# Last attention: four maximum units of a group move to the score banks, copied by ScalarE and folded on GpSimd

## The chip, the cores and the metric

One Trainium2 core runs the whole program in one launch. The metric is the device time of that launch in microseconds. The kernel before was timed three times: 1482.65, 1487.79 and 1488.82 us, median 1487.79 us. Engines: TensorE (PE; PEld is its weight load), VectorE (DVE), ScalarE (ACT), GpSimd (POOL), SyncE (SP, which issues DMAs).

## The reference

The program is a two-layer decoder on x of 4 x 512 x 256, each sublayer followed by a layer norm: attention, cross attention and a mixture of experts, then causal attention with rotary embedding, cross attention over a context of 1601 keys, and a tree of leaves. Only the last cross attention ("xa" in the kernel) is touched:

```python
def _L1_xattn_ref(q, k, v, Wq, bq, Wk, bk, Wv, bv, Wo, bo):   # 16 heads of 16
    qh = (q @ Wq + bq).reshape(B, LQ, HEADS, D_K).transpose(0, 2, 1, 3)
    kh = (k @ Wk + bk).reshape(B, LKV, HEADS, D_K).transpose(0, 2, 1, 3)
    vh = (v @ Wv + bv).reshape(B, LKV, HEADS, D_K).transpose(0, 2, 1, 3)
    scores = jnp.einsum('bhqd,bhkd->bhqk', qh, kh) * scale
    attn = jax.nn.softmax(scores, axis=-1)
    out = jnp.einsum('bhqk,bhkd->bhqd', attn, vh)
    ...
```

Here q has 512 rows in each of 4 batches, k and v have 1601.

## The kernel before, in words

`heads_loop` runs the 64 heads (4 batches x 16) as 16 groups of four heads. Each group is worked on twice. The first pass finds an estimate of each query's largest score, which the softmax subtracts. The second pass computes scores again, transposed (keys on partitions, all 512 queries along the row), takes the exponential, and multiplies by the values.

**First pass, the maximum units.** The 1601 keys are cut at 0, 512, 1024, 1473 and 1601 (`cut`). A unit is (head, block of 128 queries, cut): one bf16 matmul of 512 or 449 columns (`unit` of the tensor block, L2045) into one of three PSUM banks (banks 4 to 6), and one VectorE reduction from that bank to one column (L2194). For the last 128 keys one unit takes all four query blocks (L2039, L2187). That makes 52 units for a group: 32 of 512 columns, 16 of 449, 4 of the rest. A unit may start when the unit three places before it has been reduced. When a group's units are done, VectorE reduces the 64 partial results of each partition to 16 negated maxima (`of_cuts`, L2200), GpSimd splits them into two bf16 parts (`parts`, L1994 and L1996), PE transposes them (`shift`, L2054), ScalarE copies them out (`row`, L2154), and a DMA writes them as two extra rows under the queries, so that the second pass subtracts them in its matmul.

**Second pass.** For each of 13 blocks of 128 keys ("kt"), `scores` (L2069) computes two pairs of heads, four matmuls a pair, into one of two score banks, each two PSUM banks wide (`S_PS(p)`, p even or odd: banks 0 and 1, or 2 and 3). ScalarE takes the exponential of a pair at once, 128x1024 (L2145). A pair p may start when exponential p-2 is done. `values` (L2085) multiplies the block before by its values, four heads side by side in bank 7, with float32 operands. After a group's last values ScalarE copies the output to OT (`output`, L2135).

**Row halves.** Heads 0 and 2 of a group lie on partitions from 0, heads 1 and 3 on partitions from 64 (`base(h)`). Matmuls of 48 or 50 rows on different halves can run side by side; matmuls on the same half follow each other. The values use all 128 rows.

**Order.** PE's order is written by `group(g, ...)` of the tensor block: in every kt two scores, one values, and between them, by `due(point, count)`, maximum units of the groups ahead. Group g carries units 18 to 51 of group g+1 and then units 0 to 17 of group g+2, 52 in 39 points, four in a kt. The shift of group g+1 stands after unit 4 of group g+2 (`BEHIND`). Group 0 carries 65 units, group 14 has no group g+2 and carries 34, group 15 none. VectorE runs the units in the same order, with `of_cuts(g-1)` after unit 0 of group g. GpSimd's queue holds for each group the reload of values (`reload_v`, L1968) and then `parts`. SP reloads queries and keys when a group's scores are done. The order of units is that of `units_of_cuts`.

Of the kernel before, what the change touches and what calls it, by code (L numbers as in the profile page):

```python
# [34 lines left out]
P = 128  # L35
# [1735 lines left out]


LEFT = 128


def units_of_cuts(cuts):
# [51 lines left out]
def heads_loop(nc, env, name, hb, OT, keys=None, queries=None):  # L1828
# [13 lines left out]
    CUTS = len(cut) - 1  # L1842
    if causal:
        units = [(h, qt, 0) for h, qt in CAUSAL_UNITS]
    else:
        units = units_of_cuts(CUTS)
    U = len(units)
    R1 = UNIT_BANKS
    EARLY = U if causal else 18
    LEAD = U if causal else 5  # L1850
# [13 lines left out]

    def at(g, n):

        return g * U + n + (max(g - 1, 0) + (n > BEHIND and g > 0))

    def shift_at(g):

# [12 lines left out]
    with ExitStack() as c:  # L1883
# [17 lines left out]
        if not causal:  # L1901
            s_cuts = sem(name + "_cuts")
            s_mrow = sem(name + "_mrow")
            s_xb = sem(name + "_xb")
        s_step = sem(name + "_step")
        s_mh = sem(name + "_mh")
        s_2 = sem(name + "_2")
# [9 lines left out]
        with nc.Block() as block:  # L1917
# [44 lines left out]
            @block.gpsimd  # L1962
            def _(pool):
                def load_v(g, u):
                    full = NK // P
                    if causal and g % G == 0:
                        keys.landed(pool, g // G)
                    pool.dma_start(Vg[:, u, 0:full, :],  # L1968
                                   hb.vp[g][0:full * P, :].rearrange("(k p) n -> p k n", p=P)).then_inc(s_v[u], 16)
                    if full < KT:  # L1970
                        pool.dma_start(Vg[0:rows(full), u, full, :], hb.vp[g][full * P:NK, :]).then_inc(s_v[u], 16)

                def reload_v(g, u):
# [24 lines left out]
                if not causal:
                    parts(0)
                    for t in range(T):  # L2000
                        last = pool.tensor_tensor(env.x[:, t, :], env.x[:, t, :], env.w["x_bo"], ALU.add)
                    last.then_inc(s_xb, 1)
                    pool.wait_ge(s_xb, 1)
                    for g in range(1, GROUPS):
                        if 2 <= g <= GROUPS - R + 1:
                            reload_v(g - 2, (g - 2) % R)
                        parts(g)
                    return
                for n in keys.rest:
                    keys.split.pool_lo(pool, n)  # L2010
                pool.wait_ge(keys.split.s_lo, keys.rest[-1] + 1)
                for u in range(hb.RING, R):
                    hb.ones(pool, u).then_inc(s_ones, 1)
                pool.wait_ge(s_ones, R - hb.RING)
                for g in range(GROUPS):
                    for kt in range(KT):
                        triangle(g, kt)
                        if kt == 1 and 1 <= g <= GROUPS - R:
                            reload_v(g - 1, (g - 1) % R)

            @block.tensor
            def _(pe):
# [7 lines left out]
                def unit(g, u, n, first):  # L2030

                    if n == 0:
                        pe.wait_ge(hb.s_kq[u], 16 * hb.LOADS * (first + 1))
                    bank_free(at(g, n))
                    h, qt, e = units[n]
                    tile, to, out = base(h), place(h, 0), bank(at(g, n))
                    if qt is None:
                        for t in range(TB):
                            last = pe.matmul(out[:, t * LEFT:(t + 1) * LEFT],  # L2039
                                             hb.q(u)[tile:tile + HALF, to, t * P:(t + 1) * P],  # L2040
                                             hb.k(u)[tile:tile + HALF, to, cut[e]:NK], start=True, stop=True,
                                             tile_position=(tile, 0))
                    else:
                        width = (qt + 1) * P if causal else cut[e + 1] - cut[e]
                        last = pe.matmul(out[:, 0:width], hb.q(u)[tile:tile + HALF, to, qt * P:(qt + 1) * P],  # L2045
                                         hb.k(u)[tile:tile + HALF, to, cut[e]:cut[e] + width], start=True, stop=True,
                                         tile_position=(tile, 0))
                    last.then_inc(s_1, 1)
# [6 lines left out]
                              start=True, stop=True).then_inc(s_1, 1)  # L2055

                def scores(g, u, kt, h, first):
                    p = (kt * G + h) // 2
                    if p == 0:
                        pe.wait_ge(s_mq[u], 32 * (first + 1))  # L2060
                    if g or p >= 2:
                        pe.wait_ge(s_exp, g * PAIRS + (p - 1))
                    r = rows(kt)
                    w_ = L - q0(kt)
                    out = lambda j: S_PS(p)[0:r, j, 0:w_]
                    for half in range(2):
                        for j in range(2):
                            tile, to, depth = base(j), place(h, half), HALF + 2 * (half == 0)
                            last = pe.matmul(out(j), hb.k(u)[tile:tile + depth, to, kt * P:kt * P + r],  # L2069
                                             hb.q(u)[tile:tile + depth, to, q0(kt):L], start=(half == 0),  # L2070
                                             stop=(half == 1), tile_position=(tile, 0))
                    last.then_inc(s_2, 1)

                def values(g, u, kt, first):

                    r = rows(kt)
                    if kt == 0:
                        pe.wait_ge(s_v[u], 16 * VLOADS * (first + 1))
                        pe.wait_ge(s_ot, g + 1)
                    if causal:  # L2080
                        pe.wait_ge(s_tri, g * KT + (kt + 1))
                    else:
                        pe.wait_ge(s_exp, g * PAIRS + (kt + 1) * (G // 2))
                    for h in range(G):
                        last = pe.matmul(O_PS[h * VW:(h + 1) * VW, q0(kt):L], Vg[0:r, u, kt, h * VW:(h + 1) * VW],  # L2085
                                         Pr[0:r, (u * KT + kt) % PR, h, 0:L - q0(kt)], start=(kt == 0), stop=(kt == KT - 1),
                                         tile_position=(0, h * VW))
                    last.then_inc(s_pv, 1)

                def group(g, u, first, before, ahead):  # L2090
# [5 lines left out]
                    for kt in range(KT):  # L2096
                        for turn in range(TURNS):
# [14 lines left out]
                                    shift(g + 1)  # L2112
                            if ahead == 1 and point == LAST_POINT:
                                shift(g + 1)

                for n in range(U):
                    if not causal and n in project_at:
                        block_, k = project_at[n]
                        queries.project(pe, block_, queries.ps(block_), (k,))
# [12 lines left out]
            def _(act):  # L2132
# [4 lines left out]
                def group(g, u, before):  # L2137
                    for kt in range(KT):
# [1 line left out]
                        r = rows(kt)  # L2140
                        w_ = L - q0(kt)
                        for h in range(0, G, 2):
                            p = (kt * G + h) // 2
                            act.wait_ge(s_2, g * PAIRS + (p + 1))
                            act.activation(Pr[0:r, (u * KT + kt) % PR, h:h + 2, 0:w_], S_PS(p)[0:r, :, 0:w_], ACT.Exp,  # L2145
                                           scale=SCALE).then_inc(s_exp, 1)
                        if kt == 0 and before:
                            output(g - 1)
                        if not causal and kt == ROW_AT and g + 1 < GROUPS:
                            row(g + 1)  # L2150

# [27 lines left out]
            def _(dve):  # L2179
                def unit(g, n):  # L2180

                    h, qt, e = units[n]
                    dve.wait_ge(s_1, at(g, n) + 1)
                    src = bank(at(g, n))
                    col = h % 2 * COLS // 2 + h // 2 * TB
# [8 lines left out]
                        dve.tensor_reduce(part[:, g % 2, col + qt, e:e + 1], src[:, 0:cut[e + 1] - cut[e]], AX, ALU.max).then_inc(s_1free, 1)  # L2194

                def of_cuts(g):
                    dve.wait_ge(s_1free, reduced(at(g, U - 1)))
                    if g >= 2:
                        dve.wait_ge(s_mh, g - 1)
                    dve.tensor_reduce(mx[:, g % 2, :], part[:, g % 2, :, :], AX, ALU.max, negate=True).then_inc(s_cuts, 1)  # L2200
# [11 lines left out]
                    dve.tensor_copy(mrow[:, :], M_PS(g)).then_inc(s_1free, 1)  # L2212

                for g in range(GROUPS):
                    for n in range(U):
                        if g or not causal:
                            unit(g, n)
                        if causal and (g, n) in rest_after:
# [592 lines left out]
```

## Time and profile before

| | |
|---|---|
| median of three runs | 1487.79 us |
| the profiled execution's own time | 1489.09 us |
| its span (first to last instruction) | 1487.1 us |
| PE, DVE, ACT, POOL busy, share of the span | 92%, 71%, 52%, 22% |
| xa units' reductions (L2194), 768 | 462.7 us busy, 662 ns each |
| xa exponentials (L2145), 416 | 403.4 us busy, 1021 ns each |

The xa loop runs from about 861 to 1400 us. Read its rows by group: from one `of_cuts` to the next is one period of the loop. Busy shares of PE are upper bounds, since the ends of matmuls are modelled and matmuls overlap; where PE stands at nearly 100% it must be read instruction by instruction.

### The profile page before, as it was taken

The numbers are of one execution on the slowest core, as the hardware profiler recorded it, in microseconds if no ns is written. First come the engines' busy times: TensorE is split into PE (matmuls) and PEld (weight loads), VectorE is DVE, ScalarE is ACT, GpSimd is POOL, SyncE is SP. The second block draws the span as 40 slices with busy tenths as digits, with TensorE's granted clock in tenths as the row PEclk, the third lists the DMA queues.
The fourth block names the chain that finished last, engine by engine and source line by source line (L and its number), as shares of the span: only waits on it lengthen the run. The fifth ranks groups of instructions, "written<-read, shape, count | busy, mean of one in ns | idle before, by whom it ended". The sixth has DMA issues, their size and how long they took to land. (4 is left out here: it accounts for less than half of the span.)

```text
span 1487.1 us, 24888 instructions
## 1 busy us (share of the span) xinstructions
PE 1369.3 (92%) x9358; PEld 762.8 (51%) x9358; DVE 1059.4 (71%) x2351; ACT 774.8 (52%) x1067; POOL 321.7 (22%) x407
## 2 busy tenths in 40 slices
PE   6898899989999989869998889999999999999996
PEld 3565578756899886423335422333333333333285
DVE  4887466662122128968994799999999999997077
ACT  2344266631111112336763316888888888888754
POOL 3110322243000017743335440000000000000011
PEclk9999799999999999969999869999999999999999
DMA  9548533346889842674422650343222343220001
GB/s 341 194 134 246 171 122 128 122 165 226 299 279 302 272 152 79 215 222 143 131 66 60 177 164 2 85 102 80 67 67 68 86 101 80 68 67 2 1 1 57
DMA packets 152841, 198.68 MB, mean 134 GB/s; under 512 B 15723, under 2 KB 124799, under 8 KB 152594
## 3 DMA queue, kind: packets, MB, share of 16 engines
q1 hardware_dynamic: 141004, 165.34, 36.7%
q0 software_dynamic: 9200, 29.64, 6.4%
q10 hardware_dynamic: 2518, 2.13, 0.4%
q8 instruction: 74, 1.21, 0.4%
q14 instruction: 45, 0.37, 0.1%
HBM read 136.08 MB, written 60.70 MB: 132 GB/s over the span
## 5 line engine op out<-in xcount | busy, mean ns | idle before, releaser
L2194 DVE TENSOR_REDUCE xa_part<-psum 128x1 f32<-128x512 f32 (+1 forms) x768 | 462.7, 662 | 20.4 <-PE psum L2045 18.6
L2145 ACT ACTIVATE xa_P<-psum 128x1024 f32<-128x1024 f32 (+1 forms) x416 | 403.4, 1021 | 103.3 <-PE psum L2069 102.6
L2069 PE MATMUL psum<-sa_Q,xa_K 48*128 48x512 bf16 (+3 forms) x1664 | 267.0, 381 | 3.9 <-DMA sa_Q<-xa_mrow 2.9
L2045 PE MATMUL psum<-xa_K,sa_Q 48*128 48x512 bf16 (+1 forms) x768 | 239.3, 388 | 4.4 <-DVE xa_part L2194 1.5
L2085 PE MATMUL psum<-xa_P,xa_V 128*32 128x512 f32 (+1 forms) x1664 | 222.6, 607 | 0.4 <-ACT xa_P L2145 0.4
L2045 PEld LDWEIGHTS psum<-xa_K,sa_Q 48*128 48x128 bf16 x768 | 59.2, 94 | 232.5 <-DVE xa_part L2194 160.8
L2069 PEld LDWEIGHTS psum<-sa_Q,xa_K 48*128 48x128 bf16 (+3 forms) x1664 | 105.6, 97 | 68.7 <-ACT xa_P L2145 20.7
L2191 DVE CUSTOM_DVE_ANT_0 psum<-psum,cf_sb 128x512 f32<-128x512 f32 (+1 forms) x240 | 111.5, 520 | 18.3 <-PE psum L2045 17.5
L1334 PEld LDWEIGHTS psum<-xtT,wgu 128*128 128x128 f32 x992 | 115.5, 192 | 5.8 <-issue 4.6
L1334 PE MATMUL psum<-xtT,wgu 128*128 128x128 f32 x992 | 115.9, 275 | 1.4 <-issue 0.8
L2145 ACT ACTIVATE sa_P<-psum 128x1024 f32<-128x1024 f32 (+3 forms) x128 | 83.4, 702 | 49.1 <-PE psum L2069 49.1
L1483 DVE TENSOR_TENSOR ht<-sgt,psum 128x512 f32<-128x512 f32 x31 | 21.3, 688 | 114.1 <-ACT sgt L1386 114.1
L1386 ACT ACTIVATE sgt<-psum 128x512 f32<-128x512 f32 x31 | 18.5, 597 | 132.6 <-PE psum L1334 132.6
L212 POOL TENSOR_TENSOR t_rstd<-t_ve,mhalf 128x2 f32<-128x2 f32 (+1 forms) x36 | 27.6, 768 | 229.3 <-DVE t_ve L207 229.1
L2045 PE MATMUL psum<-sa_K,sa_Q 48*128 48x512 bf16 (+1 forms) x240 | 64.7, 321 | 12.1 <-PEq L1556 5.5
L2069 PE MATMUL psum<-sa_Q,sa_K 50*128 50x256 bf16 (+7 forms) x512 | 63.9, 308 | 4.0 <-DMA sa_Q<-sa_mrow 2.6
L1994 POOL CAST xa_mh<-xa_mx 128x16 bf16<-128x16 f32 x16 | 3.1, 197 | 293.0 <-DVE xa_mx L2200 266.8
L2085 PEld LDWEIGHTS psum<-xa_P,xa_V 128*32 128x32 f32 (+1 forms) x1664 | 32.9, 108 | 53.5 <-issue 50.6
L634 PE MATMUL psum<-a_in_sb,xT_sb 128*128 128x384 f32 x128 | 48.5, 526 | 12.9 <-DMA xT_sb<-in_xT 10.1
L1215 PE MATMUL psum<-xT_sb,big_weights 128*128 128x512 f32 x128 | 58.8, 614 | 0.7 <-PEq L937 0.7
L1981 POOL TENSOR_SCALAR_AFFINE_SELECT sa_P<-sa_P 128x512 f32<-128x512 f32 x64 | 40.6, 634 | 86.6 <-ACT sa_P L2145 86.6
L1344 PE MATMUL psum<-wdn,ht 128*128 128x256 f32 x248 | 58.7, 380 | 0.6 <-DVE yt L1490 0.6
(250 smaller groups left out, 2140.7 us busy)
## 6 DMA issues: line engine op xcount, KB each, us to landing
wgu<-in_f_gu SPq DMA_DIRECT2D x31, 1024.0 KB, 6.3
xa_K<-kx SPq DMA_DIRECT2D x192, 100.1 KB, 4.9
wdn<-in_f_dn SPq DMA_DIRECT2D x31, 512.0 KB, 6.5
vx<-xv_v SPq DMA_DIRECT2D x48, 256.0 KB, 3.3
xa_V<-vx POOLq DMA_DIRECT2D x16, 768.0 KB, 6.5
sa_Q<-qs SPq DMA_DIRECT2D x64, 96.0 KB, 2.3
sa_K<-ks SPq DMA_DIRECT2D x64, 96.0 KB, 2.3
sa_Q<-qx SPq DMA_DIRECT2D x64, 96.0 KB, 2.3
```

Source lines behind the costliest of these rows:

```text
L212: pool.tensor_tensor(self.rstd[:, u, :], self.ve[:, u, :], self.env.mhalf[:, 0:self.tc], ALU.pow).then_inc(self.s_rstd, 1)
L634: pe.matmul(o, env.xT[:, k, t * P:(t + 1) * P], w["a0_in"][:, k, cols], start=(k == 0), stop=False)
L1215: last = pe.matmul(o, w[name][:, k, f * P:(f + 1) * P], env.xT[:, k, c * L:(c + 1) * L], start=(k == 0), stop=(k == KD - 1))
L1334: last = pe.matmul(GU(j)[:, f * P:(f + 1) * P], wgu[:, u, k, f * P:(f + 1) * P], xtT[:, u, k, :], start=(k == 0), stop=(k == KD - 1))
L1344: last = pe.matmul(Y_PS[:, 0:D], ht[:, u, f, :], wdn[:, u, f, :], start=(f == 0), stop=(f == FC - 1))
L1981: pool.affine_select(square, square, [[0, G], [1, P]], ALU.is_ge, 0.0, base=0, channel_multiplier=-1).then_inc(s_tri, 1)
L2045: last = pe.matmul(out[:, 0:width], hb.q(u)[tile:tile + HALF, to, qt * P:(qt + 1) * P], hb.k(u)[tile:tile + HALF, to, cut[e]:cut[e] + widt ...
L2069: last = pe.matmul(out(j), hb.k(u)[tile:tile + depth, to, kt * P:kt * P + r], hb.q(u)[tile:tile + depth, to, q0(kt):L], start=(half == 0), ...
L2085: last = pe.matmul(O_PS[h * VW:(h + 1) * VW, q0(kt):L], Vg[0:r, u, kt, h * VW:(h + 1) * VW], Pr[0:r, (u * KT + kt) % PR, h, 0:L - q0(kt)], ...
L2145: act.activation(Pr[0:r, (u * KT + kt) % PR, h:h + 2, 0:w_], S_PS(p)[0:r, :, 0:w_], ACT.Exp, scale=SCALE).then_inc(s_exp, 1)
L2191: dve.tensor_tensor_reduce(src[:, 0:k1], src[:, 0:k1], env.later[:, L - k1:L], 1.0, -3e38, ALU.add, ALU.max, mx[:, g % 2, col + qt:col + q ...
L2194: dve.tensor_reduce(part[:, g % 2, col + qt, e:e + 1], src[:, 0:cut[e + 1] - cut[e]], AX, ALU.max).then_inc(s_1free, 1)
```

## The change

In the xa loop, the units (head 0 or 1, query block 0, cut 0 or 1), four of the 52, are taken out of the list for all groups but group 0, which keeps its 52. Their matmuls are computed as two pairs in the score banks, a pair after kt 0 and a pair after kt 1 of the group before (`fold_units`). Each pair takes a place in the order of pairs, so that the group has 28 instead of 26. ScalarE copies each pair, 128x1024, to SBUF, over constants that are no longer used (`fold`). GpSimd folds: the second copy b against the first copy a as a + max(b - a, 0), in three instructions; then the upper half of each head's 512 against the lower half, and once more, which leaves 128 per head. One VectorE reduction takes these to the four partial results, before `of_cuts`. The list of units is 48 long, so `due` spreads 48 over 39 points.

```diff
+        first_units = units_of_cuts(CUTS)
+        units = [(h, qt, e) for h, qt, e in first_units if not (h < 2 and qt == FOLD_QT and e < 2)]
...
+    FOLDS = () if causal else FOLD_AFTER
+    PAIRS += len(FOLDS)
+    pair_of = lambda g, kt, h: (kt * G + h) // 2 + sum(after < kt for after in FOLDS) * (g + 1 < GROUPS)
...
+                def folds(g):
+                    for e in range(2):
+                        pool.wait_ge(s_exp, (g - 1) * PAIRS + pair_of(g - 1, FOLD_AFTER[e], 2) + 2)
+                    a, steps, wide = fold[:, 0], 3 * FOLDINGS * (g - 1), BANK
+                    b = fold[:, 1]
+                    for n in range(FOLDINGS):
+                        pool.tensor_tensor(b, b, a, ALU.subtract).then_inc(s_fold, 1)
+                        pool.wait_ge(s_fold, steps + 3 * n + 1)
+                        pool.tensor_scalar(b, b, 3e38, 0.0, ALU.min, ALU.max).then_inc(s_fold, 1)
+                        pool.wait_ge(s_fold, steps + 3 * n + 2)
+                        pool.tensor_tensor(a, a, b, ALU.add).then_inc(s_fold, 1)
+                        if n < FOLDINGS - 1:
+                            pool.wait_ge(s_fold, steps + 3 * n + 3)
+                            wide //= 2
+                            a, b = fold[:, 0, :, 0:wide], fold[:, 0, :, wide:2 * wide]
...
+                        folds(g)
                         parts(g)
...
+                def fold_units(g, u, e, first):
+
+                    p = pair_of(g, FOLD_AFTER[e], 2) + 1
+                    if e == 0:
+                        pe.wait_ge(hb.s_kq[(u + 1) % R], 16 * hb.LOADS * (first + (u + 1) // R + 1))
+                    pe.wait_ge(s_exp, g * PAIRS + (p - 1))
+                    v = (u + 1) % R
+                    for h in range(2):
+                        tile, to = base(h), place(h, 0)
+                        last = pe.matmul(S_PS(p)[:, h, 0:BANK], hb.q(v)[tile:tile + HALF, to, FOLD_QT * P:(FOLD_QT + 1) * P],
+                                         hb.k(v)[tile:tile + HALF, to, cut[e]:cut[e + 1]], start=True, stop=True,
+                                         tile_position=(tile, 0))
+                    last.then_inc(s_2, 1)
...
+                        if kt in FOLDS and ahead >= 1:
+                            fold_units(g, u, FOLDS.index(kt), first)
...
                         if kt == 0 and before:
                             output(g - 1)
+                        if kt in FOLDS and g + 1 < GROUPS:
+                            p = pair_of(g, kt, 2) + 1
+                            if g:
+                                act.wait_ge(s_cuts, g + 1)
+                            act.wait_ge(s_2, g * PAIRS + (p + 1))
+                            act.activation(fold[:, FOLDS.index(kt)], S_PS(p), ACT.Copy).then_inc(s_exp, 1)
...
                 def of_cuts(g):
-                    dve.wait_ge(s_1free, reduced(at(g, U - 1)))
+                    dve.wait_ge(s_1free, reduced(at(g, count(g) - 1)))
+                    if g:
+                        dve.wait_ge(s_fold, 3 * FOLDINGS * g)
+                        dve.tensor_reduce(part[:, g % 2, FOLD_QT:FOLD_QT + COLS // 2 + 1:COLS // 2, 0:2],
+                                          fold[:, 0, :, 0:BANK >> (FOLDINGS - 1)].rearrange("p h (e k) -> p h e k", e=2),
+                                          AX, ALU.max).then_inc(s_folded, 1)
+                        dve.wait_ge(s_folded, g)
```

PE in a middle group before, from the last values of the group before (the row of 32x512 x4, sa_Q holds the queries, L2069 the scores, L2045 and L2039 the units):

```order
L2085 MATMUL psum<-xa_P,xa_V 32x512 x4
L2045 MATMUL psum<-xa_K,sa_Q 128x449
L2039 MATMUL psum<-xa_K,sa_Q 128x128 x4
L2069 MATMUL psum<-sa_Q,xa_K 128x512 x4
L2039 MATMUL psum<-xa_K,sa_Q 128x128 x4
L2069 MATMUL psum<-sa_Q,xa_K 128x512 x4
L2045 MATMUL psum<-xa_K,sa_Q 128x512
L2085 MATMUL psum<-xa_P,xa_V 32x512 x4
L2045 MATMUL psum<-xa_K,sa_Q 128x449
L2045 MATMUL psum<-xa_K,sa_Q 128x512
L2069 MATMUL psum<-sa_Q,xa_K 128x512 x4
```

The same place now (L2128 values, L2098 scores, L2074 units, L2112 the new pairs):

```order
L2128 MATMUL psum<-xa_P,xa_V 32x512 x4
L2074 MATMUL psum<-xa_K,sa_Q 128x449
L2112 MATMUL psum<-xa_K,sa_Q 128x512 x2
L2098 MATMUL psum<-sa_Q,xa_K 128x512 x4
L2074 MATMUL psum<-xa_K,sa_Q 128x512
L2098 MATMUL psum<-sa_Q,xa_K 128x512 x4
L2074 MATMUL psum<-xa_K,sa_Q 128x512 x2
L2128 MATMUL psum<-xa_P,xa_V 32x512 x4
L2074 MATMUL psum<-xa_K,sa_Q 128x449
L2112 MATMUL psum<-xa_K,sa_Q 128x512 x2
L2098 MATMUL psum<-sa_Q,xa_K 128x512 x4
```

A new pair stands in front of the scores of kt 1 and another in front of those of kt 2. The second scores of kt 1 and of kt 2 are now the pairs that have to wait for the new copies.

ScalarE around the end of a group before (L2145 exponentials, 65x1024 is the last kt, then kt 0 of the next group, its output copy L2135, and L2154 the row of maxima):

```order
L2145 ACTIVATE xa_P<-psum 128x1024 x4
L2145 ACTIVATE xa_P<-psum 65x1024 x2
L2145 ACTIVATE xa_P<-psum 128x1024 x2
L2135 ACTIVATE OT<-psum 128x512
L2145 ACTIVATE xa_P<-psum 128x1024 x18
L2154 ACTIVATE xa_mrow<-psum 32x128
```

And now (L2190 exponentials, L2180 output, L2199 the new copies into the region of cf_sb, L2205 the row):

```order
L2190 ACTIVATE xa_P<-psum 65x1024 x2
L2190 ACTIVATE xa_P<-psum 128x1024 x2
L2180 ACTIVATE OT<-psum 128x512
L2199 ACTIVATE cf_sb<-psum 128x1024
L2190 ACTIVATE xa_P<-psum 128x1024 x2
L2199 ACTIVATE cf_sb<-psum 128x1024
L2190 ACTIVATE xa_P<-psum 128x1024 x16
L2205 ACTIVATE xa_mrow<-psum 32x128
```

The first copy stands between the output copy and the exponentials of kt 1, the second between those of kt 1 and those of kt 2.

## Rows read from the trace of the kernel before

**Rows 1.** Windows: a middle group, most of group 15, group 0.
```profile
core 0: us, PE busy (x) PEld busy (x) DVE busy (x) ACT busy (x) POOL busy (x), PEclk, DMA share, GB/s
934.60:966.40 31.80, 31.60 (x275) 11.37 (x273) 31.27 (x54) 25.81 (x29) 2.02 (x5) 1.00 0.32 75
1377.90:1400.00 22.10, 21.43 (x170) 4.07 (x168) 0.00 (x0) 20.27 (x22) 0.00 (x0) 1.00 0.00 1
894.00:935.00 41.00, 39.21 (x295) 12.50 (x298) 38.12 (x65) 25.95 (x28) 2.61 (x6) 0.94 0.07 21
```
**Rows 2.** Timeline, POOL: the parts of maxima of two groups.
```profile
start us, us, engine line op out<-in xcount [idle before <-releaser]
1080.23 0.20 POOL L1994 CAST xa_mh<-xa_mx 128x16 bf16<-128x16 f32 x1 [17.70 <-DVE xa_mx L2200]
...
1112.04 0.20 POOL L1994 CAST xa_mh<-xa_mx 128x16 bf16<-128x16 f32 x1 [17.71 <-DVE xa_mx L2200]
1112.33 0.21 POOL L1996 TENSOR_TENSOR xa_mh<-xa_mx,xa_mh 128x16 bf16<-128x16 f32 x1
```
**Rows 3.** Lines by form, 934 to 1348 us (13 groups): VectorE and ScalarE.
```profile
line engine op names shapes xcount | busy us, mean ns | idle before us <-releasers
L2194 DVE TENSOR_REDUCE xa_part<-psum 128x1 f32<-128x512 f32 x416 | 261.6, 681 | 0.0
L2194 DVE TENSOR_REDUCE xa_part<-psum 128x1 f32<-128x449 f32 x209 | 128.2, 624 | 7.0 <-PE psum L2045 5.7
...
L2145 ACT ACTIVATE xa_P<-psum 128x1024 f32<-128x1024 f32 x313 | 303.4, 1021 | 71.8 <-PE psum L2069 71.5
```
**Rows 4.** Timeline, PE, one kt of a middle group.
```profile
1098.56 1.06 PE L2085 MATMUL psum<-xa_P,xa_V 128*32 128x512 f32 x8
1099.55 0.39 PE L2045 MATMUL psum<-xa_K,sa_Q 48*128 48x449 bf16 x2
1099.76 0.81 PE L2069 MATMUL psum<-sa_Q,xa_K 50*128 50x512 bf16 x5
...
1100.96 0.64 PE L2085 MATMUL psum<-xa_P,xa_V 128*32 128x512 f32 x4
```
**Rows 5.** Timeline, PE, at a group's end: last values, kt 1, first values.
```profile
1091.32 1.06 PE L2085 MATMUL psum<-xa_P,xa_V 65*32 65x512 f32 x8
...
1093.18 0.60 PE L2069 MATMUL psum<-sa_Q,xa_K 50*128 50x512 bf16 x3
...
1093.74 0.64 PE L2085 MATMUL psum<-xa_P,xa_V 128*32 128x512 f32 x4
```
**Rows 6.** Timeline, ACT, the same stretch (kt 0, output, kt 1).
```profile
1090.81 1.94 ACT L2145 ACTIVATE xa_P<-psum 128x1024 f32<-128x1024 f32 x2 [0.45 <-PE psum L2069]
1092.64 0.60 ACT L2135 ACTIVATE OT<-psum 128x512 f32<-128x512 f32 x1
1093.26 1.94 ACT L2145 ACTIVATE xa_P<-psum 128x1024 f32<-128x1024 f32 x2
```
**Rows 7.** Timeline, group 15, without units: ACT and the PE loads behind it.
```profile
1377.66 3.88 ACT L2145 ACTIVATE xa_P<-psum 128x1024 f32<-128x1024 f32 x4
1379.67 0.12 PEld L2069 LDWEIGHTS psum<-sa_Q,xa_K 50*128 50x128 bf16 x4 [0.67 <-ACT xa_P L2145]
```
**Rows 8.** Timeline around the shift of a middle group.
```profile
1111.77 0.21 DVE L2200 TENSOR_REDUCE xa_mx<-xa_part 128x16 f32<-128x64 f32 x1
...
1113.32 0.23 PE L2054 MATMUL psum<-cb_sb,xa_mh 128*32 128x128 bf16 x1 [0.20 <-DVE xa_part L2194]
```
**Rows 9.** Lines by form, POOL, whole program.
```profile
L1981 POOL TENSOR_SCALAR_AFFINE_SELECT sa_P<-sa_P 128x512 f32<-128x512 f32 x64 | 40.6, 634 | 86.6 <-ACT sa_P L2145 86.6
L353 POOL TENSOR_TENSOR sqk_whole<-sqk_ta,sqk_tb 128x512 f32<-128x512 f32 x16 | 22.2, 1392 | 9.8 <-DVE sqk_tb L334 9.5
L2001 POOL TENSOR_TENSOR x_sb<-x_sb,x_bo_sb 128x256 f32<-128x256 f32 x16 | 10.9, 715 | 0.0
```
**Rows 10.** Waits, 900 to 1390 us: PE's loads of units behind VectorE.
```profile
PEld psum L2045 <- DVE xa_part L2194: 136.2, 171, 0.8
```

More of the change, by code:

```diff
@@ L1773 @@
 LEFT = 128
+FOLD_QT = 0
+FOLD_AFTER = (0, 1)
+FOLDINGS = 3
 def units_of_cuts(cuts):
@@ L1844, in heads_loop @@
         units = [(h, qt, 0) for h, qt in CAUSAL_UNITS]
+        first_units = units
     else:
-        units = units_of_cuts(CUTS)
-    U = len(units)
+        first_units = units_of_cuts(CUTS)
+        units = [(h, qt, e) for h, qt, e in first_units if not (h < 2 and qt == FOLD_QT and e < 2)]
+    U0, U = len(first_units), len(units)
+    count = lambda g: U if g else U0
+    FOLDS = () if causal else FOLD_AFTER
+    PAIRS += len(FOLDS)
+    pair_of = lambda g, kt, h: (kt * G + h) // 2 + sum(after < kt for after in FOLDS) * (g + 1 < GROUPS)
     R1 = UNIT_BANKS
@@ L1865, in at @@
     def at(g, n):
-        return g * U + n + (max(g - 1, 0) + (n > BEHIND and g > 0))
+        return n if g == 0 else U0 + (g - 1) * U + n + (g - 1) + (n > BEHIND)
     def shift_at(g):
@@ L1904, in heads_loop @@
             s_xb = sem(name + "_xb")
+            s_fold = sem(name + "_fold")
+            s_folded = sem(name + "_folded")
+            fold = env.cf[:, CF_FIRST:CF_FIRST + 4 * BANK].rearrange("p (e h k) -> p e h k", e=2, h=2)
         s_step = sem(name + "_step")
@@ L2034, in unit @@
                     bank_free(at(g, n))
-                    h, qt, e = units[n]
+                    h, qt, e = units[n] if g else first_units[n]
                     tile, to, out = base(h), place(h, 0), bank(at(g, n))
@@ L2057, in scores @@
                 def scores(g, u, kt, h, first):
-                    p = (kt * G + h) // 2
+                    p = pair_of(g, kt, h)
                     if p == 0:
@@ L2082, in values @@
                     else:
-                        pe.wait_ge(s_exp, g * PAIRS + (kt + 1) * (G // 2))
+                        pe.wait_ge(s_exp, g * PAIRS + pair_of(g, kt, 2) + 1)
                     for h in range(G):
@@ L2114, in group @@
                                 shift(g + 1)
-                for n in range(U):
+                        if kt in FOLDS and ahead >= 1:
+                            fold_units(g, u, FOLDS.index(kt), first)
+                for n in range(U0):
                     if not causal and n in project_at:
@@ L2142, in group @@
                         for h in range(0, G, 2):
-                            p = (kt * G + h) // 2
+                            p = pair_of(g, kt, h)
                             act.wait_ge(s_2, g * PAIRS + (p + 1))
@@ L2180, in unit @@
                 def unit(g, n):
-                    h, qt, e = units[n]
+                    h, qt, e = units[n] if g else first_units[n]
                     dve.wait_ge(s_1, at(g, n) + 1)
@@ L2214, in _ @@
                 for g in range(GROUPS):
-                    for n in range(U):
+                    for n in range(count(g)):
                         if g or not causal:
```

## The prediction

> **What bounds the kernel now.** I read the windows by stage first, then the lines by form of the xa loop, then single rows of the timeline, because here the shares don't decide. In a middle group VectorE is busy 31.27 of 31.80 us and PE 31.60, both full; ScalarE 25.81, GpSimd 2.02 [rows 1]. The period is 1112.04 - 1080.23 = 31.81 us [rows 2]. The waits list PE's loads behind the units' reductions with 136.2 us [rows 10]; taken alone it says that VectorE is the bound and that every unit taken from it pays. Three things speak against that. First, VectorE's own idle time in 13 groups is 7.0 us, and it ends on PE [rows 3]: it is VectorE that waits in the end. Second, PE has no hole in a kt. It is: values at 1098.56, next matmul at 1099.55, scores from 1099.76, next values at 1100.96 [rows 4]. That is 2.40 us: 1.0 us of values, the rest for 8 score matmuls and 4 units, 12 matmuls on two row halves, so 6 slots one behind the other. 1100.96 - 1099.55 = 1.41; a matmul of 512 columns takes its half 0.22 us (four of scores on two halves take 0.44, as 1099.76 less 1099.55 is one slot of 0.21), so 6 slots are 1.32 and 0.09 is left for the change to values. Third, the loads wait for the values in front of them anyway: group 15 has no units at all, and its loads wait 0.67 us "for ScalarE" in the same place [rows 7]. So PE paces, at 13 x 2.41 = 31.3 us, and 0.5 us comes on top around the shift, where PE does wait for a bank of VectorE's (0.20 us idle at 1113.32) [rows 8].
>
> ScalarE is the other half of PE's loop. There are two score banks, and a pair may start only when the exponential two pairs back is done. Four exponentials in a row take 3.88 us, 0.97 each; the first after a gap counts 1.02 [rows 3, 7]. At kt 0 the output copy already fills ScalarE's gap: kt 0's two from 1090.81, output 1092.64 to 1093.24, kt 1's two from 1093.26, without idle time [rows 6].
>
> **The change part by part.**
>
> Four units less on VectorE, 14 groups. A reduction of 512 columns costs one step of (261.6 / 416 =) 0.63 us, so 2.5 us a group leave, and one reduction of 256 elements comes. Its price lies between 0.21 us (64 elements, [rows 8]) and 0.63; I take 0.4 and 0.15 for its two handshakes. VectorE is relieved by about 2 us a group, which off the path is worth nothing by itself.
>
> PE's work: nothing is taken away. The same four matmuls run, two side by side: 2 slots of 0.22 in kt 0 and 1. The units that remain are 48 in 13 kt, three or four in each. Three units still take 6 slots (4 + 2 on one half, 4 + 1 on the other), so a kt with three is not shorter. Where three fall on one half it takes 7, 0.22 us more. Taking units 0, 2, 3 and 4 out of the list breaks the alternation of halves: by the heads in the list I count this in kt 9 and kt 10, and once after kt 1, where two units of one half stand in a row behind the values. That makes +0.6 us a group. Around the shift the 0.5 us may go (VectorE has slack) or double (the fold's reduction stands in front of `of_cuts`): -0.5 to +0.5, I take -0.1. Remainder: +0.5 a group, from -0.5 to +1.2.
>
> The two copies: this is the main term. A copy of 128x1024 from PSUM is the shape of the exponential, so 1.02 us [rows 3]. No row shows this copy to SBUF; the output copy, half its size, takes 0.60 [rows 6], which bounds it by 1.2 above and by 0.97 below. I follow the group that ends at 1091.32 [rows 5, 6]:
> - Copy 1 waits in ScalarE's queue behind the output copy: 1093.28 to 1094.30. Its matmuls were ready at about 1092.9.
> - The exponentials of kt 1 wait behind it: from 1094.33 instead of 1093.26, the second ends at 1096.27.
> - The second scores of kt 1 need copy 1's bank. They start at 1094.30 + 0.07 = 1094.37 (the 0.07: exponential ends 1377.66 + 1.94 = 1379.60, PE's load at 1379.67 [rows 7]) instead of 1093.18 [rows 5]. PE issues in order, so units and values behind them wait too. Then 0.44 of scores, one slot of units, 0.09: values at 1095.12 instead of 1093.74. Late by 1.38.
> - Values to 1096.12, a short unit and the second pair on the same half 0.41, 0.16 to its end: 1096.69. ScalarE has been idle since 1096.27 and starts copy 2 at 1096.80, until 1097.82.
> - The first scores of kt 2 run meanwhile; the second need copy 2's bank: 1097.89, plus 0.44, 0.22 and 0.09: values at 1098.64. Before, they stood one kt after 1093.74: 1096.15. Late by 2.49.
> - Kt 2's exponentials end at 1099.80, before the second scores of kt 3 ask for the bank (about 1100.3). From here on PE paces again, and ScalarE has 0.4 us a kt, so nothing is won back, for PE has no slack.
>
> So 2.45 us a group (2.2 to 2.9 with the bounds of the copy). With the remainder: 2.95 x 14 groups (1 to 14) = 41.3 us.
>
> Group 0 is another case: 65 units in 41 us, VectorE busy 38.12 [rows 1], so VectorE paces at 5 units a kt, 3 us, and two exponentials and a copy fit into 3 us. Four units less are 2.5 us, the fold's reduction costs some of it: -1.5 us (-2.5 to +2.5). Group 15 has no copies. The first 52 units stay.
>
> GpSimd: nine instructions a group on 1024, 512 and 256 elements. Two inputs: 512 take 1.39, 256 take 0.72 [rows 9], so 1024 take 2.8: 4.9 us a series, 9.8 for the two series. The third kind has one input; no row shows it. One-input affine selects take 0.63 for 512 [rows 9], so 2.2 a series; as dear as two inputs it would be 4.9. Handshakes 9 x 0.09 [rows 2]. Together 12.8 to 15.5 us from the end of copy 2 at 1097.8. `of_cuts` ran at 1111.77 [rows 8] and comes about 2.5 us later and one turn (a third of a kt) earlier: 1113.9. There are 16.1 us, so it is hidden, at worst with 0.6 us left. The Trainium skill (GPSIMD Engine Reference, section 3.1, "Elementwise — side-by-side cycle accounting") has about 2.6 cycles an element for two inputs and 1.03 for one; by its figures the nine would take an estimated 9.3 us and a start each, shorter than by the rows, and still hidden. The values' reload stands in GpSimd's queue before the folds and isn't delayed; `parts` stands behind them and needs `of_cuts` anyway.
>
> The other waits: ScalarE's wait for `of_cuts` of the group is met a group earlier; the wait for the next group's keys was met when its units began.
>
> **Sum.** +41.3 - 1.5 = +39.8. Against the profiled execution: 1489.1 + 39.8 = 1528.9; it lies 1.3 us over the median of the three runs, so 1527.6 for a median, 1528. Its own range: 14 x (2.2 - 0.5) - 2.5 = +21 to 14 x (2.9 + 1.2) = +57, which I narrow to 1513 to 1542 since not all ends meet.
>
> **Rivals.**
> - VectorE paces after all. Then units taken from it pay and the waits of PE are slack. For it: 31.27 of 31.80 us busy, 136.2 us of waits. Against it: its idle time ends on PE. It would save 2.0 us of reductions less 0.15, down to ScalarE's floor: 28 x 1.0 + 0.6 + 0.25 and the gaps, about 30.0. So -1.8 x 15 = -27 us: 1461. This is the faster side; it decides as soon as PE's matmuls can go on under the copies. Chance 0.08.
> - The copies' waits are half taken up (the units standing in front of the scores run during them, the shift's 0.5 us goes and the halves cost nothing): the two cancel nearly. 14 x (1.0 - 0.5) = +7 and less: 1485 to 1495. It needs a second score bank free when copy 1 runs, and there is none. Chance 0.05.
> - GpSimd is late. If the nine take 18.5 us (inputs slowed by VectorE's traffic, which no row shows), `of_cuts` waits 2.4 us, three banks fill, PE stops: 14 x 2.4 = 34 more: 1562. Chance 0.10.
> - PE's clock falls in the new holes. Group 15 has ScalarE's holes in every kt and the granted clock is 1.00; at the low clock of group 0's beginning it is below, 0.94 over the group [rows 1]. If two kt a group ran at 1.2 instead of 2.4 GHz, each would cost up to its own 2.4 us again; by half of that, 14 x 2.4 = 34 more: 1562. Chance 0.04. The Trainium skill (TensorE: Matmul & The Clock Gate, "A second HAM failure mode: psum-queue depth-cycling") tells of a clock that swings where PE idles shortly between groups of matmuls while it cycles through PSUM; the row of group 15 doesn't bear it out.
>
> **Chances and range.** Forecast 0.73, the rivals 0.08, 0.05, 0.10, 0.04. A change under 0.5%, 7.4 us, can't be told from none. Faster 0.09, same 0.05, slower 0.86. The range must leave out no more than 0.2: 1509 to 1547 leaves out the first two rivals and most of the last two, which hold 0.25 with the nearer ends inside.
>
> **What would show it.** Right: the exponentials' count per group unchanged, two copies of about 1.02 us behind output and behind kt 1; PE idle about 1 us before the second scores of kt 1 and kt 2, ended by ScalarE's copy; values 3.8, 3.5 us apart at the group's start and 2.4 after; VectorE busy about 29 of 35 us a group; period 34.5 to 35.2. GpSimd's last fold ends before VectorE's reduction of it asks. Wrong: a period under 31.8 with VectorE still above 97% (first rival); VectorE's idle time ended by GpSimd (third); PEclk under 1.00 in the loop (fourth). If the values stand 2.4 us apart at kt 1 and 2, the main term is wrong.

## The result, and the profile after

Slower: median 1521.79 us against 1486.68 us, ratio 1.0241, 95% interval 1.0222 to 1.0260, +35.1 us. The forecast was 1528, +39.8. The profiled execution took 1521.9 us, its span 1520.1 us against 1487.1.

The windows of a whole middle group, of group 14 and of group 0, after (columns as in [rows 1]):

```profile
894.00:935.00 41.00, 38.61 (x310) 12.10 (x308) 37.26 (x64) 29.42 (x32) 15.07 (x14) 1.00 0.22 54
964.50:999.20 34.70, 33.30 (x275) 10.59 (x273) 29.81 (x50) 27.57 (x32) 12.87 (x13) 1.00 0.30 72
1380.70:1411.90 31.20, 29.93 (x244) 8.13 (x242) 15.96 (x27) 25.88 (x30) 11.23 (x11) 1.00 0.01 2
```

A middle group takes 34.68 us instead of 31.82. No engine is full any more: PE has 1.4 us without work, VectorE 4.9. PEclk is 1.00, so the holes did not cost clock. VectorE's lines by form over groups 1 to 13, to set beside [rows 3]:

```profile
L2245 DVE TENSOR_REDUCE xa_part<-psum 128x1 f32<-128x512 f32 x364 | 237.7, 686 | 54.0 <-PE psum L2074 49.9
L2245 DVE TENSOR_REDUCE xa_part<-psum 128x1 f32<-128x449 f32 x208 | 125.4, 618 | 7.6 <-PE psum L2074 7.5
L2251 DVE TENSOR_REDUCE xa_part<-cf_sb 128x4 f32<-128x256 f32 x13 | 5.3, 411 | 0.0
```

Its idle time rose from 7 us to over 60, and ends on PE. VectorE was relieved, and the relief turned into waiting. Where the time went stands in the timeline of PE at a group's end, the place of [rows 5]. A stretch is the time from the start of one kt's values (L2128) to that of the next:

```profile
1099.61 1.06 PE L2128 MATMUL psum<-xa_P,xa_V 65*32 65x512 f32 x8
1100.61 0.36 PE L2074 MATMUL psum<-xa_K,sa_Q 48*128 48x449 bf16 x1
1100.61 0.57 PE L2112 MATMUL psum<-xa_K,sa_Q 48*128 48x512 bf16 x2
1101.08 0.61 PE L2098 MATMUL psum<-sa_Q,xa_K 50*128 50x512 bf16 x4
...
1102.48 0.61 PE L2098 MATMUL psum<-sa_Q,xa_K 50*128 50x512 bf16 x4 [0.58 <-ACT cf_sb L2199]
...
1103.24 1.06 PE L2128 MATMUL psum<-xa_P,xa_V 128*32 128x512 f32 x8
...
1104.24 0.57 PE L2112 MATMUL psum<-xa_K,sa_Q 48*128 48x512 bf16 x2
...
1105.99 0.61 PE L2098 MATMUL psum<-sa_Q,xa_K 50*128 50x512 bf16 x4 [0.71 <-ACT cf_sb L2199]
...
1106.75 1.06 PE L2128 MATMUL psum<-xa_P,xa_V 128*32 128x512 f32 x8
```

and of ScalarE (to [rows 6]):

```profile
1100.91 0.60 ACT L2180 ACTIVATE OT<-psum 128x512 f32<-128x512 f32 x1
1101.38 1.05 ACT L2199 ACTIVATE cf_sb<-psum 128x1024 f32<-128x1024 f32 x1
1102.29 1.98 ACT L2190 ACTIVATE xa_P<-psum 128x1024 f32<-128x1024 f32 x2
1104.91 1.02 ACT L2199 ACTIVATE cf_sb<-psum 128x1024 f32<-128x1024 f32 x1 [0.65 <-PE psum L2112]
1105.83 1.94 ACT L2190 ACTIVATE xa_P<-psum 128x1024 f32<-128x1024 f32 x2
```

Copy 1 ends at 1102.43, and the second scores of kt 1 start at 1102.48; copy 2 ends at 1105.93, and those of kt 2 start at 1105.99. Values stand 3.63 and 3.51 us apart there (forecast 3.80 and 3.52), 2.41 before. The shorter first one is ScalarE's overlap: the start after an instruction comes 0.1 us before its end (1100.91 to 1101.38, 1101.38 to 1102.29), which I had counted only between the two exponentials of a kt. PE itself stands idle for 0.58 and 0.71 us, not for the 1 us that the prediction gave as a sign; beside the hole stand the new pair's own matmuls, 0.47 us with a unit (1100.61 to 1101.08).

GpSimd's folds, after:

```profile
1106.08 2.36 POOL L2016 TENSOR_TENSOR cf_sb<-cf_sb 128x1024 f32<-128x1024 f32 x1 [3.42 <-ACT cf_sb L2199]
1108.54 1.03 POOL L2018 TENSOR_SCALAR cf_sb<-cf_sb 128x1024 f32<-128x1024 f32 x1
1109.66 2.36 POOL L2020 TENSOR_TENSOR cf_sb<-cf_sb 128x1024 f32<-128x1024 f32 x1
...
1116.83 0.74 POOL L2020 TENSOR_TENSOR cf_sb<-cf_sb 128x256 f32<-128x256 f32 x1
```

and VectorE's reduction of them:

```profile
1121.63 0.41 DVE L2251 TENSOR_REDUCE xa_part<-cf_sb 128x4 f32<-128x256 f32 x1
```

The nine take 11.5 us, from 1106.08 to 1117.57, and end 4.1 us before VectorE's reduction of them starts, without idle time in front of it. They are hidden.

### The profile page after: what moved, and what is told of

Read it like the earlier page. It is cut to its first block and busy times, and to the rows that moved or that the text cites. A ratio compares the mean times of both kernels' runs of the same rounds, so it can differ in the third digit from the quotient of the medians.

```text
span 1520.1 us, 25081 instructions
## 1 busy us (share of the span) xinstructions
PE 1384.3 (91%) x9358; PEld 748.6 (49%) x9358; DVE 1036.3 (68%) x2306; ACT 800.5 (53%) x1097; POOL 484.1 (32%) x542
## 5 line engine op out<-in xcount | busy, mean ns | idle before, releaser
L2245 DVE TENSOR_REDUCE xa_part<-psum 128x1 f32<-128x512 f32 (+1 forms) x708 | 433.4, 661 | 76.5 <-PE psum L2074 71.2
L2190 ACT ACTIVATE xa_P<-psum 128x1024 f32<-128x1024 f32 (+1 forms) x416 | 403.9, 1024 | 104.3 <-PE psum L2098 104.0
L2098 PE MATMUL psum<-sa_Q,xa_K 50*128 50x512 bf16 (+3 forms) x1664 | 284.5, 381 | 22.6 <-ACT cf_sb L2199 18.6
L2074 PE MATMUL psum<-xa_K,sa_Q 48*128 48x512 bf16 (+1 forms) x708 | 232.4, 384 | 4.0 <-PEq L2327 1.0
L2128 PE MATMUL psum<-xa_P,xa_V 128*32 128x512 f32 (+1 forms) x1664 | 222.5, 607 | 0.4 <-ACT xa_P L2190 0.4
L2074 PEld LDWEIGHTS psum<-xa_K,sa_Q 48*128 48x128 bf16 x708 | 61.9, 95 | 214.7 <-DVE xa_part L2245 171.8
L2098 PEld LDWEIGHTS psum<-sa_Q,xa_K 50*128 50x128 bf16 (+3 forms) x1664 | 93.4, 96 | 113.1 <-ACT cf_sb L2199 33.4
L2190 ACT ACTIVATE sa_P<-psum 128x1024 f32<-128x1024 f32 (+3 forms) x128 | 83.4, 702 | 48.0 <-PE psum L2098 48.0
L2016 POOL TENSOR_TENSOR cf_sb<-cf_sb 128x1024 f32<-128x1024 f32 (+2 forms) x45 | 65.5, 1456 | 67.5 <-ACT cf_sb L2199 65.2
L2074 PE MATMUL psum<-sa_K,sa_Q 48*128 48x512 bf16 (+1 forms) x240 | 64.3, 319 | 12.1 <-PEq L1556 5.5
L1406 POOL DMA_DIRECT2D yg<-yt x31 | 16.8, 543 | 182.7 <-DVE yt L1490 182.7
L1980 POOL DMA_DIRECT2D xa_V<-vx x16 | 17.3, 1083 | 171.6 <-PE psum L2128 167.1
L2098 PE MATMUL psum<-sa_Q,sa_K 50*128 50x256 bf16 (+7 forms) x512 | 63.6, 307 | 4.2 <-DMA sa_Q<-sa_mrow 2.9
L2020 POOL TENSOR_TENSOR cf_sb<-cf_sb 128x1024 f32<-128x1024 f32 (+2 forms) x45 | 65.7, 1459 | 3.7
L2128 PEld LDWEIGHTS psum<-xa_P,xa_V 128*32 128x32 f32 (+1 forms) x1664 | 32.8, 108 | 64.1 <-issue 60.0
```

The lines of the kernel that those rows point to most:

```text
L2016: pool.tensor_tensor(b, b, a, ALU.subtract).then_inc(s_fold, 1)
L2020: pool.tensor_tensor(a, a, b, ALU.add).then_inc(s_fold, 1)
```

## The experiments

The starts of the values, read instruction by instruction from each trace, give the length of each stretch. In us, for a middle group, counted from its first values to those of the next group ("last" is the stretch in which the next group's copy 1 lies, 0-1 the one with copy 2; the shift lies in 7-8):

| kernel | 0-1 | 1-2 | 2-7 (sum) | 7-8 | 8-9 | 9-10 | 10-12 (sum) | last | group | median us | ratio to before (95%) |
|---|---|---|---|---|---|---|---|---|---|---|---|
| before | 2.41 | 2.41 | 12.09 | 2.69 | 2.59 | 2.41 | 4.82 | 2.42 | 31.82 | | |
| after | 3.51 | 2.49 | 12.24 | 2.82 | 2.59 | 2.59 | 4.82 | 3.63 | 34.68 | 1521.8 | 1.0241 (1.0222 to 1.0260) |
| e1 | 2.41 | 2.41 | 12.09 | 2.42 | 2.42 | 2.41 | 4.82 | 2.42 | 31.37 | 1478.8 | 0.9948 (0.9934 to 0.9963) |
| e2 | 2.38 | 2.49 | 12.24 | 2.64 | 2.59 | 2.59 | 4.81 | 2.41 | 32.15 | 1487.2 | 1.0003 (0.9993 to 1.0012) |
| e3 | 2.40 | 2.37 | 12.38 | 2.64 | 2.40 | 2.46 | 4.84 | 2.40 | 31.88 | 1483.8 | 0.9970 (0.9960 to 0.9980) |
| e4 | 3.53 | 2.41 | 12.09 | 2.69 | 2.59 | 2.41 | 4.82 | 3.64 | 34.16 | 1517.8 | 1.0205 (1.0190 to 1.0220) |

The rows' sums differ from the group by rounding. Each ratio compares with the kernel before, run beside that experiment. e1, e2, e3 and e5 leave part of the maxima out of the computation; of these only the times are used.

**e1_light_reduce: VectorE alone lighter.**

```diff
-src[:, 0:cut[e + 1] - cut[e]]
+src[:, 0:64 if g and h < 2 and qt == 0 and e < 2 else cut[e + 1] - cut[e]]
```

> The kernel before; only VectorE's reductions of the four units (head 0 or 1, query block 0, cut 0 or 1) of groups 1 to 15 read 64 of their 512 columns (those maxima are then over fewer keys). PE, ScalarE and the order are the same. Theory (PE paces, VectorE only around the shift): between no change and the 0.5 us a group of the shift, 0 to -7 us. Rival (VectorE paces): a reduction of 64 columns takes about 0.2 us instead of 0.63, so -1.7 us a group, -24 to -26 us.

Measured -0.5%, some 9 us (1478.8 against 1487.5). The four reductions fell to 0.22 us each, 1.8 us a group less for VectorE. VectorE's lines by form over groups 1 to 13:

```profile
L2194 DVE TENSOR_REDUCE xa_part<-psum 128x1 f32<-128x512 f32 x364 | 228.3, 681 | 0.0
L2194 DVE TENSOR_REDUCE xa_part<-psum 128x1 f32<-128x449 f32 x208 | 127.5, 623 | 21.0 <-PE psum L2045 20.5
...
L2194 DVE TENSOR_REDUCE xa_part<-psum 128x1 f32<-128x64 f32 x52 | 10.4, 220 | 3.2 <-PE psum L2045 3.2
```

Its idle time is 24.2 us instead of 7.0. Of each group only the two stretches around the shift moved, 5.28 to 4.84 us; all others kept their length to the hundredth. So VectorE holds PE back around the shift, by 0.44 us, and nowhere else. In 13 groups that is 5.7 us; the rest of the 9 lies outside them and is not explained here. The rival "VectorE paces" would have had -24 us.

**e2_drop4: the four units gone, nothing in their place.** (`FOLDS = ()`, no `folds(g)`.)

> The four units are left out of groups 1 to 15 altogether: no matmuls, no copies, no fold, 48 units in the changed kernel's order (their maxima are stale). Theory: a kt with three units takes the same six slots as one with four, and the disturbed order of row halves costs up to 0.6 us a group, the shift gives back up to 0.5: a middle group 31.6 to 32.1 us, the whole -5 to +3 us, though a thirteenth of the units is gone. Rival (VectorE paces): -2.5 us a group, -37 us. A count of PE's matmuls alone: two slots of 0.22 us a group, -6 us.

Measured 1.0003, with four matmuls and four reductions fewer in each group. The middle group even grew by 0.33 us. Group 0 shortened by 2.3 us (40.39 to 38.09): 1.7 us from its second stretch on, where VectorE paces, and 0.6 us in its first, which differs between traces with the same units too (4.62 us before, 4.35 in e4). A kt with three units takes 2.38 to 2.50 us, one with four 2.41: it is not shorter by a slot of 0.22.

**e3_drop4_turns: as e2, row halves in strict turn.** (The 48 units are listed even head, odd head, even head, ...)

> As e2_drop4, but the 48 units are listed with the row halves in strict turn (head even, head odd, ...). Theory of the halves: against e2_drop4 0.3 to 0.6 us a group less, -4 to -8 us, so -4 to -12 us against before; kt 9 and kt 10 fall from 2.6 to 2.4 us. Rival (halves cost nothing): the same as e2_drop4.

Measured 1483.8, against 1487.2 of e2. Stretch 8-9 fell from 2.59 to 2.40 us, 9-10 from 2.59 to 2.46 and 1-2 from 2.49 to 2.37; 2-7 rose by 0.14. On balance the order of the halves costs 0.27 us a group, half of what I had put for it.

**e4_copies_only: all 52 units on VectorE, pairs and copies added, nothing folded.** (`units = first_units`; no `folds(g)`; no reduction of the fold.)

> All 52 units stay on VectorE, and the two new pairs with their copies are added; nothing is folded and nothing reads the copies. Theory (copies and two score banks stall PE): 2.45 us a group at the first two kt, perhaps a bit more around the shift, +34 to +42 us against before, most of the changed kernel's loss; values 3.6 and 3.5 us apart at kt 0 and 1. Rival (the loss is of GpSimd, the fold's reduction and the order of units): +0 to +10 us.

Measured +2.05%, 30 us at the medians, a little under what I expected. The group is before's, hundredth by hundredth, except for the two stretches with copies: +1.22 and +1.12, together 2.35 us (31.82 to 34.16). This is 82% of the changed kernel's 2.86 us a group, with GpSimd, fold and order of units taken out. PE waits in the same place for the same reason:

```profile
969.51 0.41 PE L2111 MATMUL psum<-xa_K,sa_Q 48*128 48x512 bf16 x2
...
971.09 0.61 PE L2097 MATMUL psum<-sa_Q,xa_K 50*128 50x512 bf16 x4 [0.52 <-ACT cf_sb L2198]
```

**e5_short_copies: the copies take 64 columns of each half.**

```diff
-act.activation(fold[:, FOLDS.index(kt)], S_PS(p), ACT.Copy)
+act.activation(fold[:, FOLDS.index(kt), :, 0:64], S_PS(p)[:, :, 0:64], ACT.Copy)
```

> The changed kernel, but each copy takes 64 of the 512 columns of both halves (the fold then works on old data). Nothing else moves. Theory (it is the length of the copy between a pair and the scores two places on): a copy of 128 elements takes about 0.3 us instead of 1.02; the wait before the second scores of kt 1 falls from 0.6 us to nothing, that of kt 2 to about 0.1; of 2.35 us a group about 1.3 go, the two slots of the pairs and a rest stay: -18 us against the changed kernel, about 1504. Rival (the place in PE's order costs, not the copy): the same as the changed kernel, 1522.

Measured 1501.8 us (ratio to before 1.0105, 1.0079 to 1.0131), group 33.19 us, so 20 us of 35 gone. ScalarE and PE at copy 2:

```profile
995.78 0.28 ACT L2199 ACTIVATE cf_sb<-psum 128x128 f32<-128x128 f32 x1 [0.44 <-PE psum L2112]
996.21 1.94 ACT L2190 ACTIVATE xa_P<-psum 128x1024 f32<-128x1024 f32 x2 [0.16 <-PE psum L2098]
```
```profile
995.11 0.57 PE L2112 MATMUL psum<-xa_K,sa_Q 48*128 48x512 bf16 x2
995.39 0.72 PE L2098 MATMUL psum<-sa_Q,xa_K 50*128 50x512 bf16 x4
...
996.11 0.61 PE L2098 MATMUL psum<-sa_Q,xa_K 50*128 50x512 bf16 x4
```

The copy is 0.28 us and PE's second scores start 0.05 us behind its end, 996.06. They still wait, but less, which the waits of PE's loads for the copies show (us in all, times, longest), first in the changed kernel, then in e5:

```profile
PEld psum L2098 <- ACT cf_sb L2199: 31.9, 28, 1.2
```
```profile
PEld psum L2098 <- ACT cf_sb L2199: 9.7, 27, 0.4
```

The two stretches are 2.76 and 2.89 us. So the stretch follows the copy's length: 0.74 us less of copy gives 0.75 and 0.74 us less of stretch. Against e2, where nothing is copied (2.38 and 2.41), 0.86 us a group are left. The prediction put 0.44 of that down to the pairs' own matmuls; no run here separates them from the rest of the wait.

**e6_after_1_2: pairs behind kt 1 and 2** (`FOLD_AFTER = (1, 2)`).

> The changed kernel with the pairs behind kt 1 and 2 instead of 0 and 1, away from the output copy. In the copies' run kt 0 cost 1.23 us and kt 1 1.12 us. Theory: the output copy adds only the difference, so 2 x 1.12: -0.1 to -0.3 us a group, -1 to -5 us against the changed kernel. Rival (the output copy in front is what makes copy 1 dear): -0.5 us a group or more, -8 to -15 us.

A miss. 1523.9 us (1.0251, 1.0227 to 1.0274), the group 34.69 us as before the move. The two stretches are 3.51 and 3.73, where e2 without copies has 2.38 and 2.49, so 1.13 and 1.24 us. Taken with the changed kernel (1.22 behind kt 0, 1.13 behind kt 1) and with e7 below (1.24 behind kt 2, 1.16 behind kt 4), the price goes with the place. Copy 1 did get 0.09 us cheaper away from the output copy, as the theory had it, and copy 2 got 0.11 dearer behind kt 2. So the output copy is at most 0.1 us of the price; why kt 2 is the dearer place I did not isolate.

**e7_after_2_4: pairs behind kt 2 and 4.**

> The changed kernel with the pairs behind kt 2 and 4. The nine folds take 11.5 us there and end 4.1 us before VectorE asks. Copy 2 now ends about 7.1 us later. Theory (the rival of the late GpSimd, made true): VectorE waits about 3 us for GpSimd in each group, the three unit banks fill, PE loses 2 to 3 us of it: +28 to +42 us against the changed kernel, 1550 to 1564. Other theory (VectorE's slack takes the wait up): 1518 to 1526.

The direction was right, the size was not, twice the 42 us that the theory had as its most: 1610.2 us, ratio 1.0838 (1.0810 to 1.0866), +88 us against the changed kernel. VectorE waits for GpSimd as foreseen:

```profile
1116.48 0.42 DVE L2251 TENSOR_REDUCE xa_part<-cf_sb 128x4 f32<-128x256 f32 x1 [3.38 <-POOL cf_sb L2020]
```

and PE, out of unit banks, stands still 2.99 us. Then something comes on top, in the timeline of PE and the windows (columns as in [rows 1]):

```profile
1117.75 0.60 PE L2074 MATMUL psum<-xa_K,sa_Q 48*128 48x512 bf16 x1 [2.99 <-DVE xa_part L2245]
...
1119.91 1.94 PE L2128 MATMUL psum<-xa_P,xa_V 128*32 128x512 f32 x8
```
```profile
1112.00:1116.00 4.00, 2.76 (x23) 0.74 (x19) 1.10 (x2) 2.96 (x3) 3.58 (x6) 1.00 0.00 0
1116.00:1119.00 3.00, 1.25 (x6) 0.36 (x7) 2.48 (x6) 0.00 (x0) 0.80 (x3) 0.71 0.01 3
1119.00:1122.00 3.00, 3.00 (x15) 0.45 (x13) 1.11 (x2) 1.17 (x2) 0.00 (x0) 0.50 0.00 0
1122.00:1126.00 4.00, 4.00 (x26) 1.22 (x24) 2.61 (x5) 2.05 (x2) 0.00 (x0) 0.74 0.01 2
```

The granted clock falls to 0.50, 1.2 GHz, at the end of the hole and stays there for 6.9 us in this group:

```profile
1117.20:1124.10 6.90, 6.35 (x26) 1.57 (x27) 4.00 (x7) 1.94 (x3) 0.41 (x2) 0.51 0.01 2
```

The values take 1.94 us instead of 1.06. The stretch is 6.97 us and the next 4.64, where the changed kernel has 2.82 and 2.59: 6.2 us a group, 3 of waiting and, as what is left, about 3 of clock.

**e8_after_turns: the changed kernel with the halves in turn.**

> The changed kernel with the 48 units in strict turn of row halves. In the kernel without the four units this took a middle group from 32.15 to 31.88 us. Theory: the same here, -0.27 us a group, -3 to -5 us against the changed kernel, about 1518. Rival (under the copies' waits the halves don't matter): no change, 1522.

1518.6 us (1.0227, 1.0203 to 1.0251), -3.2 us against the changed kernel's own 1521.8. The intervals of the two overlap, so the medians alone don't tell them apart. The middle groups of the traces do, 34.52 against 34.68 us: -0.16, not the -0.27 of the theory, because the stretch of the shift grew from 2.82 to 2.94.

**e9_unit_banks: two units copied from their own banks, score banks left alone.** The copies of units 0 and 8 stand behind kt 8 and kt 10:

```diff
+                        if not causal and kt in COPY_AT and g + 2 < GROUPS:
...
+                            act.activation(fold[:, i], bank(at(g + 2, COPIED[i])), ACT.Copy).then_inc(s_copy, 1)
```

> A version that may beat both: the kernel before, but of groups 2 to 15 units 0 and 8 (head 0, query block 0, cuts 0 and 1; the list's units 4 and 8 are exchanged) are copied by ScalarE out of their unit bank, 128x512, at kt 8 and kt 10 of the group two before, folded by GpSimd into 128 elements, and reduced by VectorE behind unit 24. PE's order and the score banks are as before. Theory: the copy lies in ScalarE's 0.46 us of gap and costs 0 to 0.15 us each; VectorE is lighter by 0.6 us just in front of of_cuts, and lightening it there gave 0.44 us a group at most: -0.4 to +0.2 us a group, -6 to +3 us against before, 1481 to 1490. Rival (any copy on ScalarE stalls PE as in the changed kernel): +10 us and more.

1492.5 us, 1.0040 (1.0024 to 1.0056): a little slower than before, +7 us, beyond the +3 of the theory and short of the rival's +10. No version here that computes everything beats the kernel before. The group is 32.26. The shift kept its 2.69 and 2.59, but that does not say that a lighter VectorE gives nothing there, for now the copy at kt 8 holds PE in the same place. It ends at 1145.58 (0.60 us from 1144.98), and the load of the unit that takes the same bank comes behind it:

```profile
1145.63 0.09 PEld L2073 LDWEIGHTS psum<-xa_K,sa_Q 48*128 48x128 bf16 x1 [0.58 <-ACT cf_sb L2182]
```

Which of e1's four units gave its 0.44 us is therefore open. The copy at kt 10 cost:

```profile
1151.01 0.39 PE L2073 MATMUL psum<-xa_K,sa_Q 48*128 48x512 bf16 x1 [0.18 <-ACT cf_sb L2182]
```

A unit waits for its bank, since the copy runs behind both exponentials (from 1150.35), and the stretch is 2.76 instead of 2.41. Per copied unit this is cheaper than through the score banks (0.44 us for two units against 2.35 for four), but it is still a loss.

## Why the prediction was right, by its steps

- *PE paces, VectorE is full but not the bound.* Right, shown by e1 and e2: 1.8 us a group less on VectorE gave 0.44, and four units fewer gave nothing. The 0.5 us of the shift is VectorE's, also shown by e1 (0.44).
- *The copies, 2.45 us a group.* Measured 2.35 in e4; the 0.1 is the overlap of starts on ScalarE. e5 shows that 1.5 of it goes with the copy's length.
- *Remainder, +0.5 us.* Measured 0.51 (34.68 - 31.82 - 2.35), but in other parts than I had it: 0.33 is what the group grows by without the four units (e2), of which 0.27 goes with the halves in turn (e3); I had 0.6 for the halves and -0.1 for the shift. The shift grew from 2.69 to 2.82, while it should have shrunk by the lighter VectorE (e2: 2.64): 0.18 more than in e2. e4, with the copies and without the fold, keeps it at 2.69 as before, so the 0.18 belong to the fold; that it is its reduction and handshakes in front of `of_cuts` is argued, not shown. That these parts add up to the 0.5 of the forecast is luck.
- *The groups added up, +41.3 - 1.5 = +39.8.* Measured from values to values, groups 1 to 13 lengthened by 2.86 us each, group 14 by 1.51 (29.63 to 31.14), and group 0 shortened by 0.70: 13 x 2.86 + 1.51 - 0.70 = 38.0 us. The sum counts a group's copy 1 to that group, while the stretches have it at the end of the group before. In its own terms groups 1 to 14 gave 39.9 us, not 41.3: 2.86 for thirteen of them and 2.72 for group 14, whose second half has no units and takes 1.97 to 2.28 us a stretch in both kernels, where the sum had 2.95 for all. Group 0 gave -1.9, not -1.5, though its last stretch, with copy 1 of group 1, grew from 2.42 to 3.63.
- *The rest of the way to 33 us of span* is, as far as the traces tell, not the change. The first values of group 0 start at 890.2 us instead of 894.3 and the tail is 1.0 us shorter. In the ten other traces, before and experiments, the first values start between 888.7 and 894.3. The scatter is there before the change can act: `of_cuts` of group 0, with all 52 units in front of it in every kernel, starts at 883.2 before, at 879.4 after, and between 877.8 and 883.1 in the experiments. So the profiled pair shows 33 us where the groups make 38; the medians, 35.1 us apart, lie between.
- *GpSimd hidden, 12.8 to 15.5 us.* Hidden, but 11.5 us. The means I scaled from were too dear: 512 elements of two inputs took 1.27 here against the 1.39 of [rows 9], and 1024 took 2.36, not twice 1.39. The one-input kind took 1.03 for 1024. The room was 15.7 us from the end of copy 2 (1105.93) to VectorE's reduction (1121.63). The prediction had 16.1; its own terms (1111.77 + 2.5, less a third of a kt) make 1113.5 and not 1113.9, so 15.7. The Trainium skill's per-element figures (GPSIMD Engine Reference, section 3.1, "Elementwise — side-by-side cycle accounting") of 2.6 and 1.03 cycles gave an estimated 9.3 us plus starts. The trace took 2.2 us more than that: each instruction has a part that does not depend on its elements, about 0.2 us (twice 1.28 less 2.36, twice 0.61 less 1.03), and the eight gaps between the nine are 0.7 us together.
- *The clock rival.* Not in the changed kernel, PEclk 1.00 with holes of 0.6 and 0.7 us. The row that the prediction leant on, group 15, could not carry this: the 0.67 us there are a wait of PE's weight loads, and PE's own hole in front of the same scores, in the kernel before, was 0.18 us (below). e7 shows the rival at work, with a hole of 3.0 us. No run here has a hole between 0.7 and 3.0 in the loop, so where it begins is open.

```profile
1379.67 0.61 PE L2069 MATMUL psum<-sa_Q,xa_K 50*128 50x512 bf16 x4 [0.18 <-ACT xa_P L2145]
```

Open: why the pair behind kt 2 costs 1.24 us and the one behind kt 1 1.13 (e6), why a kt with three units in e2 and e3 takes up to 2.50 instead of 2.41, and how the 0.86 us that stay with short copies divide (e5).

## What to carry to other kernels

An engine at 98% may still be the one that follows: ask which engine its idle time ends on, and take load from it alone once before building a path around it. Here 1.8 us a group off VectorE, at 98%, gave 0.44. Work moved into a pair of buffers that another loop lives on makes that loop wait for it, here for a copy of 1.0 us on an engine with 0.45 us of slack a kt, twice a group, and the work taken away elsewhere paid nothing back. Where matmuls run in pairs on row halves, count slots and not matmuls: a kt with three units was no shorter than one with four, and putting the halves in turn was worth up to 0.19 us in a kt, nearly a slot.

## What the runs showed of the hardware

A hole of 3.0 us on PE was followed by 6.9 us at a granted clock of 0.50 (e7), so that a wait of 3 us cost 6. Two holes of 0.6 and 0.7 us in every group left it at 1.00. ScalarE's copy of 128x1024 from PSUM to SBUF takes 1.02 us, of 128x512 0.60 and of 128x128 0.28, and its successor can start 0.1 us before its end. GpSimd's float32 tensor-tensor takes 2.36, 1.28 and 0.73 us for 1024, 512 and 256 elements, its tensor-scalar with two operations 1.03, 0.61 and 0.40.
